# Regrouping the third gating cycle of a gated cross-attention block, with its second layer in three passes

## The chip, the cores and the metric

The kernel runs on one core of a Trainium2 chip. The metric is the device time of one execution, in microseconds (us); lower is better. A core has TensorE (PE, matrix products into the accumulator memory PSUM), VectorE (DVE), ScalarE (ACT), GpSimd (POOL) and SyncE (SP, which here only issues transfers). Each engine works through its own list of instructions in order; an instruction may wait on semaphores that other engines or transfers raise.

## The reference, cut to what matters

```python
x = x + tanh(g_xattn) * attention(layernorm(x), ctx, ctx, adj, mask, ...)     # not touched
x = x + tanh(g_ffn) * ffn(layernorm(x))

def ffn(x):                                   # 4 batches of 1024 tokens, 512 features
    gf = global_net(mean over tokens of x)    # one value a batch
    out = x
    for _ in range(3):                        # three gating cycles
        h = gelu(out @ w1 + b1)               # 512 -> 512
        h = gelu(h @ w2 + b2)                 # 512 -> 256
        h = gelu(h @ w3 + b3)                 # 256 -> 128
        tf = sigmoid(h @ w4 + b4)             # 128 -> 1
        coupling = 0.1 + adaptive_range * (0.7 * gf + 0.3 * tf - 0.5) * 2
        out = out + coupling * twist(out)     # twist turns quarters of the row, with signs
    return out
```

## The kernel before, in words

The program has three phases, one after the other on every engine: projections, attention, and the last one, `ffn_phase`, which alone is touched. It runs over four batches; a batch is worked as two streams, j = 0 and j = 1, of 512 tokens each. Arrays of a stream are tiles of 128 features x 512 tokens, four tiles to 512 features.

A batch begins with the output projection of attention (`project`, 12 products for each of 8 pieces; stream 1's piece s waits for DVE's `residual` of stream 0's piece s, since they share the accumulator), goes on with layer normalisation, transposes and the first layer (`first_layer`), and ends with the three gating cycles. Since `twist` is linear and turning twice gives the negative, the first layer is computed once: A = w1 applied to x, B = w1 applied to the twisted x. Before the first cycle's gelu the sum is A. With the coupling of the first cycle in `beta` the second cycle's sum is A + beta B. With c the coupling of the second cycle, the third cycle's sum is alpha A + (beta + c) B, alpha = 1 - beta c.

In a cycle n of stream j: DVE forms the sum tile by tile into `u[j]` (`mix`), ACT applies gelu in place (`h1`), PE multiplies by w2 (`layer2`, four tiles t, two products each), ACT applies gelu (`h2_half`, twice), PE multiplies by w3 (`layer3`), ACT applies gelu (`h3_all`), PE multiplies by w4 (`layer4`, copied to all 128 rows), ACT takes tanh (`gate`), DVE makes the coefficients (`coefficients`). PE alternates the streams: it does tiles 1, 2, 3 of a turn's `layer2`, then `layer3`, then tile 0 of the next turn's `layer2`, then `layer4`. ACT's order is fixed in `batch`: in the turn of one stream it does that stream's `h2_half` twice, `h1` tile 0 of the other stream's next cycle, `h3_all`, `h1` tile 1, `gate`, and then `h1` tiles 2 and 3. No engine can take a later instruction ahead of one that waits.

In the first cycle `layer2` is three products in the fast format for each one (`three_pass`: high x high, low x high, high x low), from a rounded copy `u_hi` that ACT writes and a low part `u_lo` that DVE's `split_u` makes; `SPLIT = 1` says that only cycle 0 does so. The other two cycles use one full-precision product, which the profile shows as two records.

After the third cycle the output is written in rows. For it the coefficients are wanted as columns: ACT packs alpha and beta into one tile (`pack`), PE turns it (`columns`), DVE reads it (`gated_columns`), makes the columns of the output (`y_columns`), and finishes it piece by piece (`finish`, or `finish_base` and `finish_add` where ACT does the twisted part in `twist`: only in the last stream of the last batch).

In batch 0 POOL also finishes the last four pieces of the attention's output (`split_weighted`, five operations each, which SP loads before and stores after), while the cycles run; only after the fourth does SP go on to load the next batch's rows.

## Time and profile before

| | us |
|---|---|
| median of three runs (lowest, highest) | 1735.72 (1734.1, 1736.67) |
| profiled execution, its own time | 1736.92 |
| its span, first to last instruction | 1735.1 |
| PE busy / DVE / ACT / POOL | 1708.5 / 1443.4 / 1244.5 / 659.9 |
| `ffn_phase`, first product of batch 0 to that of batch 1 | 1244.27 to 1367.32 |
| the same, batch 1 to batch 2 | 1367.32 to 1486.57 |

The busy time of an engine is the time in which at least one of its instructions was executing. The span starts at the first instruction; all positions below are microseconds from there. A timeline row gives an instruction's start and duration; neighbours on one engine may overlap, so that what one costs its engine is the distance from its start to the next one's.

### The profile page before, as it was taken

To read this page: it belongs to the slowest core of one execution; us is meant where nothing else is said; L and a number is where in the kernel's file an instruction comes from. 1 tells how busy PE (TensorE), PEld (TensorE's weight loads), DVE (VectorE), ACT (ScalarE), POOL (GpSimd) and SP (SyncE) were. 2 spreads that over 40 slices of the span, in tenths; PEclk is the share of its full clock that TensorE was granted. 3 is DMA by queue.
4 is the path that set the end of the run, shared out by engine and by line. 5 is a ranking of instruction groups with operands and counts; after the bars stand their busy time and mean duration, and the time that the engine had idled before them with its cause. 6 is when DMAs were issued, how large, how long until landed. Compare 5 with 4: busy or idle time off the path is not lost. (4 is left out here: it accounts for less than half of the span.)

```text
span 1735.1 us, 34186 instructions
## 1 busy us (share of the span) xinstructions
PE 1708.5 (98%) x12456; PEld 1291.2 (74%) x12456; DVE 1443.4 (83%) x2554; ACT 1244.5 (72%) x2185; POOL 659.9 (38%) x590
## 2 busy tenths in 40 slices
PE   9999999999999999999999999999999999999997
PEld 7887888777777777777777777777775685774863
DVE  6554555999999999999999999999678976868868
ACT  4222223999999999999999999999574365365455
POOL 3432341423278542586432885633235010100100
PEclk9999999999999999999999999999999999999999
DMA  7778675865468665567764686455403513221101
GB/s 279 274 239 289 225 270 158 189 184 135 131 160 198 129 154 123 135 212 142 160 154 116 185 182 138 120 111 153 162 17 98 169 40 119 88 74 49 64 1 49
DMA packets 152472, 254.65 MB, mean 147 GB/s; under 512 B 17024, under 2 KB 69504, under 8 KB 152320
## 3 DMA queue, kind: packets, MB, share of 16 engines
q1 hardware_dynamic: 101936, 158.78, 28.7%
q0 software_dynamic: 49808, 92.82, 23.8%
q8 instruction: 93, 1.52, 0.4%
q10 hardware_dynamic: 576, 1.05, 0.2%
q14 instruction: 59, 0.48, 0.1%
HBM read 168.44 MB, written 84.15 MB: 146 GB/s over the span
## 5 line engine op out<-in xcount | busy, mean ns | idle before, releaser
L1021 DVE CUSTOM_DVE_ANT_0 a_neg<-a_sc_ps,am 128x1024 f32<-128x1024 f32 x512 | 621.5, 1214 | 1.4 <-PE a_sc_ps L853 1.3
L961 ACT ACTIVATE a_prob<-a_neg,a_row_min 128x1024 f32<-128x1024 f32 x512 | 585.5, 1144 | 13.9 <-DVE a_row_min L1021 7.8
L867 PEld LDWEIGHTS a_tr_ps<-ident,a_prob 128*128 128x128 f32 x4096 | 461.0, 140 | 89.2 <-issue 53.2
L867 PE MATMUL a_tr_ps<-ident,a_prob 128*128 128x128 f32 x4096 | 519.8, 274 | 0.9 <-ACT a_probT L939 0.9
L996 DVE COPY a_probT<-a_tr_ps 128x512 f32<-128x512 f32 x512 | 350.5, 685 | 36.8 <-PE a_tr_ps L867 35.3
L939 ACT ACTIVATE a_probT<-a_tr_ps 128x512 f32<-128x512 f32 x512 | 304.0, 594 | 35.2 <-PE a_tr_ps L867 16.2
L749 POOL DMA_DIRECT2D a_q_st<-q_parts x144 | 79.4, 558 | 201.2 <-PE a_sc_ps L853 165.4
L853 PE MATMUL a_sc_ps<-k_first,a_q_st 96*128 96x512 f32 x384 | 126.3, 427 | 0.1
L853 PE MATMUL a_sc_ps<-a_k_st,a_q_st 96*128 96x512 f32 x384 | 125.8, 426 | 0.0
L887 PE MATMUL a_o_ps<-a_probT,a_v 128*32 128x256 f32 x2048 | 123.6, 382 | 0.6 <-ACT a_o L950 0.6
L887 PE MATMUL a_o_ps<-a_probT,v_first 128*32 128x256 f32 x2048 | 123.8, 382 | 0.0
L1380 PE MATMUL f_acc<-f_u,f_w 128*128 128x512 f32 x256 | 116.0, 596 | 0.7 <-ACT f_u L1517 0.7
L887 PEld LDWEIGHTS a_o_ps<-a_probT,a_v 128*32 128x32 f32 x2048 | 60.5, 109 | 55.8 <-ACT a_probT L939 12.0
L887 PEld LDWEIGHTS a_o_ps<-a_probT,v_first 128*32 128x32 f32 x2048 | 60.0, 109 | 56.2 <-DVE a_probT L996 11.6
L961 ACT ACTIVATION_READ_ACCUMULATOR a_prob<-a_neg,a_row_min 128x1 f32 x512 | 97.1, 190 | 0.0
L754 POOL TENSOR_SCALAR a_m_raw<-a_m_raw 128x1024 f32<-128x1024 int32 x24 | 86.9, 3629 | 25.4 <-DMA a_m_raw<-mask 25.4
L1380 PEld LDWEIGHTS f_acc<-f_u,f_w 128*128 128x128 f32 x256 | 47.6, 190 | 61.7 <-issue 48.5
L132 POOL TENSOR_TENSOR st_o<-st_o,st_rinv 128x512 f32<-128x512 f32 x32 | 41.6, 1300 | 110.3 <-DMA st_rinv<-rinv_all 110.2
L1670 DVE TENSOR_TENSOR f_B<-f_B,f_acc 128x512 f32<-128x512 f32 x64 | 43.7, 682 | 33.6 <-PE f_acc L166 23.8
L1274 POOL TENSOR_TENSOR f_rstd<-f_var_eps,f_minus_half 128x4 f32<-128x4 f32 x8 | 10.4, 1297 | 160.6 <-DVE f_neg_mean L1647 160.6
L488 DVE SCALAR_TENSOR_TENSOR p_out_lo<-p_acc,p_bias_k,p_out_hi 128x512 fp32r<-128x512 f32 x32 | 23.7, 750 | 55.2 <-ACT p_out_hi L416 55.2
L1521 ACT ACTIVATE f_h<-f_acc,small_b 128x512 f32<-128x512 f32 x48 | 32.8, 687 | 48.6 <-PE f_acc L1380 33.7
(227 smaller groups left out, 3166.2 us busy)
## 6 DMA issues: line engine op xcount, KB each, us to landing
a_q_st<-q_parts POOLq DMA_DIRECT2D x144, 128.0 KB, 3.9
k_first<-k_parts POOLq DMA_DIRECT2D x24, 512.0 KB, 8.3
a_k_st<-k_parts POOLq DMA_DIRECT2D x24, 512.0 KB, 8.1
a_m_raw<-mask SPq DMA_DIRECT2D x24, 512.0 KB, 5.0
a_adj_raw<-adj SPq DMA_DIRECT2D x24, 512.0 KB, 5.9
k_parts<-p_out_hi SPq DMA_DIRECT2D x32, 256.0 KB, 4.2
k_parts<-p_out_lo SPq DMA_DIRECT2D x32, 256.0 KB, 6.2
v_all<-p_v_out SPq DMA_DIRECT2D x8, 1024.0 KB, 4.4
```

The costliest lines, as they stand in the source:

```text
L132: pool.tensor_tensor(w.o[:], w.o[:], w.rinv[:], ALU.mult).then_inc(w.step, 1)
L749: pool.dma_start(q_st[qb][quad * D:(quad + 1) * D], src).then_inc(q_loaded[qb], 16)
L754: pool.tensor_scalar(m_raw[:, t % 2, :].bitcast(F32), m_raw[:, t % 2, :], 0.0, -BIG, ALU.is_equal, ALU.mult).then_inc(big_ready, 1)
L853: last = pe.matmul(sc_ps[:, r % 2, half * 512:(half + 1) * 512], q_st[qb][0:STACK, h, qt * P:(qt + 1) * P], k_st[par][0:STACK, h, half * 5 ...
L867: last = pe.transpose(tr_ps[:, bank(u, half), j * P:(j + 1) * P], prob[:, r % NPROB, t * P:(t + 1) * P], ident[:])
L887: last = pe.matmul(o_ps[h * D:(h + 1) * D, 0:QB], v_sb[vpar][:, t, h * D:(h + 1) * D], probT[:, prev % 2, h, t, :], start=(t == 0), stop=( ...
L939: act.activation(probT[:, (r // UB) % 2, h, 0:4, qt * P:(qt + 1) * P], tr_ps[:, bank(u, 0), :].rearrange("p (t q) -> p t q", t=4), ACT.Cop ...
L961: act.activation(prob[:, r % NPROB, :], neg[:, r % 2, :], ACT.Exp, scale=-1.0, bias=row_min[:, r % 2:r % 2 + 1], accum_out=row_sum[:, r // ...
L996: dve.tensor_copy(probT[:, (r // UB) % 2, h, 4:8, qt * P:(qt + 1) * P], tr_ps[:, bank(u, 1), :].rearrange("p (t q) -> p t q", t=4)).then_i ...
L1021: dve.tensor_tensor_reduce(out=neg[:, r % 2, :], in0=sc_ps[:, r % 2, :], in1=am[:, 2 * qb + qt, :], scale=-1.0, scalar=3.4e38, op0=ALU.add ...
L1380: last = pe.matmul(acc[:, 2 * j + m, :], w2[:, t, m * P:(m + 1) * P], u[j][:, t, :], start=t == 0, stop=t == ET - 1)
L1670: dve.tensor_tensor(target[j][:, m, :], target[j][:, m, :], acc[:, 2 + step // 2, :], op).then_inc(shared_read, 1)
```

## The change

It touches only `ffn_phase`. In its own parts:

1. The third cycle's sum is regrouped: the second cycle's sum A + beta B is kept in `u[j]`, B - beta A is built beside it (`turned`: per tile one product beta A and one subtraction), and the third cycle's sum is u + c (B - beta A) (`third_cycle`). So that `u[j]` survives, the second cycle's gelu goes to a tile of its own, `h1_second`.
2. The coupling is formed on ACT, by a second activation behind the tanh, instead of on DVE; alpha, `cross` and the sum beta + c of full width are gone.
3. The third cycle's `layer2` is in three passes as well (`SPLIT = (0, 2)`). ACT writes gelu twice for it (`u_hi_third` and `u`), DVE makes the low part (`split_u`).
4. The split weights are copied by two transfers from POOL's queue (`keep_w2`) to a place that the next batch's attention tiles don't overwrite; those tiles' loads (`load_attention`) now wait for the copy (stream 0) or for the batch's last `layer2` (stream 1), whose `u_hi_third` lies where they go.
5. The columns no longer go through ACT and PE. SP stores one row of beta and of c to memory and loads them back as columns; DVE makes the gated columns from them with four small operations.
6. In the turn of stream 0's third cycle ACT also does the twisted part of two of the four output pieces (`twist(b, 0, 2)`, `twist(b, 0, 3)`), in all batches.

```diff
+        w2_kept = [nc.alloc_sbuf_tensor_at(f"f_w2_kept{part}", [P, ET, F2], F32R, offset=sb.offset + 4096 * part) for part in range(2)]
...
+        u_hi_third = [nc.alloc_sbuf_tensor_at(f"f_u_hi_third{j}", [P, ET, CH], F32R, offset=SB_AM + 8192 * j) for j in range(NJ)]
...
+                for j in range(NJ):
+                    sp.wait_ge(t_ready, turn(b, 1, j) + 1)
+                    for kind, row in enumerate((beta, coef)):
+                        sp.dma_start(gate_rows[b, j, kind:kind + 1], row[0:1, j, :]).then_inc(rows_stored, 16)
+                    sp.wait_ge(rows_stored, 32 * (NJ * b + j + 1))
+                    with nc.allow_non_contiguous_dma(reason="one row becomes four columns"):
+                        for kind in range(2):
+                            sp.dma_start(raw_cols[:, j, kind], gate_rows[b, j, kind].rearrange("(s p) -> p s", p=P)).then_inc(cols_loaded[j], 16)
...
         @block.gpsimd
         def _(pool):
+            def keep_w2(b):
+                pool.wait_ge(product_ready, 4 * ET * NJ * (b + 1))
+                pool.wait_ge(w2_lo_ready, b + 1)
+                for kept, tile in zip(w2_kept, (w2_hi, w2_lo)):
+                    pool.dma_start(kept[:], tile[:]).then_inc(w2_kept_loaded, 16)
...
             def load_attention(b, j, part):
                 if j == 0:
-                    pool.wait_ge(z2_ready, 2 * turn(b - 1, SPLIT - 1, 1) + 2)
+                    pool.wait_ge(z2_ready, 2 * turn(b - 1, 0, 1) + 2)
+                    pool.wait_ge(w2_kept_loaded, 32 * b)
                 else:
...
+                keep_w2(b)
...
-                    for j in (1, 0):
+                    for j in range(NJ):
                         for part in range(2):
                             load_attention(b + 1, j, part)
...
-                    if n < SPLIT:
-                        pe.wait_ge(w2_lo_ready, b + 1)
+                    if n in SPLIT:
                         pe.wait_ge(u_lo_ready, ET * turn_split(b, n, j) + t + 1)
-                        for m in range(2):
...
+                        if n in SPLIT:
+                            last = three_pass(pe, acc[:, 2 * j + m, :], w_hi[:, t, ms], w_lo[:, t, ms], high[:, t, :], u_lo[j][:, t, :],
                                               t == 0, t == ET - 1)
-                            if t == ET - 1:
-                                last.then_inc(z2_ready, 1)
-                        continue
-                    pe.wait_ge(h1_ready, ET * k + t + 1)
-                    for m in range(2):
...
             def h1(b, n, j, m):
                 k = ((CYCLES - 1) * b + n - 1) * NJ + j
+                if n == 1:
+                    act.wait_ge(product_ready, 4 * ET * NJ * (b + 1))
+                elif m == 0:
+                    act.wait_ge(z2_ready, 2 * turn(b, 1, j) + 2)
                 act.wait_ge(u_ready, ET * k + m + 1)
-                if n < SPLIT:
-                    act.activation(u_hi[j][:, m, :], u[j][:, m, :], ACT.Gelu, bias=small.b1[:, m:m + 1])
+                if n == 1:
+                    act.activation(h1_second[j][:, m, :], u[j][:, m, :], ACT.Gelu, bias=small.b1[:, m:m + 1]).then_inc(h1_ready, 1)
+                    return
+                act.activation(u_hi_third[j][:, m, :], u[j][:, m, :], ACT.Gelu, bias=small.b1[:, m:m + 1])
...
+                if n == 0:
+                    wait(act, rows_stored, 32 * NJ * b)
+                act.activation(coef[:, j, :], z4[:, j, :], ACT.Tanh, scale=0.5, bias=small.half_b4[:]).then_inc(tanh_ready, 1)
+                act.wait_ge(base_ready, b + 1)
+                act.wait_ge(tanh_ready, NJ * ((CYCLES - 1) * b + n) + j + 1)
+                act.activation((beta if n == 0 else coef)[:, j, :], coef[:, j, :], ACT.Identity, scale=small.range_3[:], bias=base[:]).then_inc(t_ready, 1)
...
-                        if other[1] == CYCLES - 1:
-                            pack(b, other[2])
+                    if n == CYCLES - 1 and j == 0:
+                        twist(b, 0, 2)
+                        twist(b, 0, 3)
...
-                add(ET - 1)
+                    dve.tensor_tensor(u[j][:, m, :], u[j][:, m, :], A[j][:, m, :], ALU.add).then_inc(u_ready, 1)
+                in_turn(scale, add)
+            def turned(b, j, tiles):
+                k = ET * (NJ * b + j)
+                dve.wait_ge(u_ready, ET * ((CYCLES - 1) * b * NJ + j + 1))
+                for m in tiles:
+                    dve.tensor_tensor(A[j][:, m, :], A[j][:, m, :], beta[:, j, :], ALU.mult).then_inc(twist_step, 1)
+                    if m > tiles[0]:
+                        subtract(j, m - 1, k)
+                subtract(j, tiles[-1], k)
+            def subtract(j, m, k):
+                dve.wait_ge(twist_step, k + m + 1)
+                dve.tensor_tensor(Bt[j][:, m, :], Bt[j][:, m, :], A[j][:, m, :], ALU.subtract).then_inc(turned_ready, 1)
+            def third_cycle(b, j):
+                k = ET * (NJ * b + j)
+                dve.wait_ge(t_ready, turn(b, 1, j) + 1)
+                dve.wait_ge(turned_ready, k + ET)
+                def scale(m):
+                    dve.tensor_tensor(Bt[j][:, m, :], Bt[j][:, m, :], coef[:, j, :], ALU.mult).then_inc(B_scaled, 1)
+                def add(m):
+                    dve.wait_ge(B_scaled, k + m + 1)
+                    dve.tensor_tensor(u[j][:, m, :], u[j][:, m, :], Bt[j][:, m, :], ALU.add).then_inc(u_ready, 1)
+                in_turn(scale, add)
             def gated_columns(b, j):
                 k = NJ * b + j
-                dve.wait_ge(cols_ps_ready, k + 1)
-                dve.tensor_scalar(cols[:, j].rearrange("p k s -> p s k"), z4[:, j, 0:2 * TT].rearrange("p (s k) -> p s k", k=2),
-                                  small.gate_f[:], None, ALU.mult).then_inc(cols_ready, 1)
+                be, c, al, both = raw_cols[:, j, 0], raw_cols[:, j, 1], cols[:, j, 0], cols[:, j, 1]
+                dve.wait_ge(cols_loaded[j], 32 * (b + 1))
+                dve.scalar_tensor_tensor(al, be, -1.0, c, ALU.mult, ALU.mult).then_inc(cols_step, 1)
+                dve.tensor_tensor(both, be, c, ALU.add).then_inc(cols_step, 1)
+                dve.wait_ge(cols_step, 2 * k + 2)
+                dve.tensor_scalar(al, al, 1.0, small.gate_f[:], ALU.add, ALU.mult).then_inc(cols_ready, 1)
...
                 dve.wait_ge(t_ready, turn(b, CYCLES - 1, j) + 1)
                 dve.tensor_scalar(c, t_cols[:, j], small.range_3[:], base[:], ALU.mult, ALU.add).then_inc(y_cols_step, 1)
-                dve.wait_ge(cols_ready, k + 1)
+                dve.wait_ge(cols_ready, 2 * k + 2)
                 dve.wait_ge(y_cols_step, done + 1)
                 dve.tensor_tensor(cross_be, c, be, ALU.mult).then_inc(y_cols_step, 1)
                 dve.tensor_tensor(cross_al, c, al, ALU.mult).then_inc(y_cols_step, 1)
...
-                    if n < CYCLES - 1:
-                        coefficients(b, n, j)
-                        mix(b, n + 1, j)
-                        if n + 1 < SPLIT:
-                            split_u(b, n + 1, j)
+                    if n == 0:
+                        second_cycle(b, j)
+                        turned(b, 0, ((0, 1, 2), (3,))[j])
+                        if j:
+                            turned(b, 1, (0, 1))
+                    elif n == 1:
+                        third_cycle(b, j)
+                        if j == 0:
+                            turned(b, 1, (2,))
+                        split_u(b, 2, j)
+                        if j == 0:
+                            turned(b, 1, (3,))
                     else:
                         gated_columns(b, j)
                         y_columns(b, j)
                         if j == 0:
-                            for s in range(TT):
-                                finish(b, 0, s)
+                            finish(b, 0, 0)
+                            finish(b, 0, 1)
+                            finish_base(b, 0, 2)
+                            finish_base(b, 0, 3)
+                            finish_add(b, 0, 2)
+                            finish_add(b, 0, 3)
             batches(dve, batch)
```

Names in the order rows: `f_u_..02` and `..08` are u[0], the next number u[1]; `w_raw` is A of stream 1; `f_B` the B of a stream; `f_h` holds the outputs of `h2_half` and `h3_all`; f_acc, f_tr and f_z are PSUM. A row ends with the size of the output, and x2 is two alike.

ACT, last batch, the turn of stream 1's second cycle, before:

```order
L1521 ACTIVATE f_h_1_18607<-f_acc,small_b_71 128x512 x2
L1517 ACTIVATE f_u_18602<-f_u_18602,small_b_70 128x512
L1525 ACTIVATE f_h_1_18607<-f_tr,small_b_72 128x512
L1517 ACTIVATE f_u_18602<-f_u_18602,small_b_70 128x512
L1530 ACTIVATE f_coef<-f_z,small_half_b_75 128x512
L1517 ACTIVATE f_u_18602<-f_u_18602,small_b_70 128x512 x2
L1541 ACTIVATE f_coef<-f_alpha 64x512
L1542 ACTIVATE f_coef<-f_beta 64x512
```


and now:

```order
L1538 ACTIVATE f_h_1_18613<-f_acc,small_b_71 128x512 x2
L1533 ACTIVATE f_u_hi_third_18600<-f_u_18608,small_b_70 128x512
L1534 ACTIVATE f_u_18608<-f_u_18608,small_b_70 128x512
L1542 ACTIVATE f_h_1_18613<-f_tr,small_b_72 128x512
L1533 ACTIVATE f_u_hi_third_18600<-f_u_18608,small_b_70 128x512
L1534 ACTIVATE f_u_18608<-f_u_18608,small_b_70 128x512
L1549 ACTIVATE f_coef<-f_z,small_half_b_75 128x512
L1552 ACTIVATE f_coef<-f_coef,f_base,small_range_77 128x512
L1533 ACTIVATE f_u_hi_third_18600<-f_u_18608,small_b_70 128x512
L1534 ACTIVATE f_u_18608<-f_u_18608,small_b_70 128x512
L1533 ACTIVATE f_u_hi_third_18600<-f_u_18608,small_b_70 128x512
L1534 ACTIVATE f_u_18608<-f_u_18608,small_b_70 128x512
```


Behind the two activations of `h2_half` stood eight instructions (four gelus, `h3_all`, the tanh and two of packing); now there are eleven (eight gelus, `h3_all`, the tanh and the second activation of the gate), and the last two of these stand before the gelus of tiles 2 and 3. The twists of part 6 come in the next turn, behind the gelus of stream 1's tiles 2 and 3 and ahead of stream 1's `h2_half`.

DVE, last batch, stream 1's third sum (all but its first two operations) and the first operation of stream 0's columns, before:

```order
L1707 TENSOR_TENSOR f_u_18603<-w_raw,f_alpha 128x512
L1708 TENSOR_TENSOR f_B_18601<-f_B_18601,f_beta 128x512
L1715 TENSOR_TENSOR f_u_18603<-f_u_18603,f_B_18601 128x512
L1707 TENSOR_TENSOR f_u_18603<-w_raw,f_alpha 128x512
L1708 TENSOR_TENSOR f_B_18601<-f_B_18601,f_beta 128x512
L1715 TENSOR_TENSOR f_u_18603<-f_u_18603,f_B_18601 128x512
L1707 TENSOR_TENSOR f_u_18603<-w_raw,f_alpha 128x512
L1708 TENSOR_TENSOR f_B_18601<-f_B_18601,f_beta 128x512
L1715 TENSOR_TENSOR f_u_18603<-f_u_18603,f_B_18601 128x512 x2
L1727 TENSOR_SCALAR f_cols<-f_z,small_gate_f 128x4x2
```


and now, the stretch from the last pieces of `turned` to the low parts of stream 1:

```order
L1724 TENSOR_TENSOR w_raw<-w_raw,f_beta 128x512
L1731 TENSOR_TENSOR f_B_18607<-f_B_18607,w_raw 128x512
L1695 TENSOR_TENSOR f_u_lo_18610<-f_u_18608,f_u_hi_third_18600 128x512 x4
L1724 TENSOR_TENSOR w_raw<-w_raw,f_beta 128x512
L1731 TENSOR_TENSOR f_B_18607<-f_B_18607,w_raw 128x512
L1739 TENSOR_TENSOR f_B_18607<-f_B_18607,f_coef 128x512 x2
L1743 TENSOR_TENSOR f_u_18609<-f_u_18609,f_B_18607 128x512
L1739 TENSOR_TENSOR f_B_18607<-f_B_18607,f_coef 128x512
L1743 TENSOR_TENSOR f_u_18609<-f_u_18609,f_B_18607 128x512
L1739 TENSOR_TENSOR f_B_18607<-f_B_18607,f_coef 128x512
L1743 TENSOR_TENSOR f_u_18609<-f_u_18609,f_B_18607 128x512 x2
L1695 TENSOR_TENSOR f_u_lo_18611<-f_u_18609,f_u_hi_third_18601 128x512 x4
```


Stream 1's third sum used to follow stream 0's with only the coefficients between, and the columns followed it; now it stands behind four low parts of stream 0 and one more pair of `turned`, and four low parts of stream 1 stand between it and the columns.

POOL, batch 0, before (`f_rstd` and `f_shift` belong to the normalisation of stream 1, `st_` tiles to `split_weighted`):

```order
L1276 TENSOR_TENSOR f_shift<-f_neg_mean,f_rstd 128x4
L1269 TENSOR_TENSOR f_pair_lo<-f_alpha,f_pair_hi 128x512 x2
L132 TENSOR_TENSOR st_o<-st_o,st_rinv 128x512
L135 TENSOR_SCALAR st_lo<-st_o 128x512
L137 TENSOR_TENSOR st_hi<-st_lo,st_o 128x512
```


and now:

```order
L1289 TENSOR_TENSOR f_rstd<-f_var_eps,f_minus_half 128x4
L1291 TENSOR_TENSOR f_shift<-f_neg_mean,f_rstd 128x4
L1284 TENSOR_TENSOR f_pair_lo<-f_pair_raw,f_pair_hi 128x512 x2
L1262 DMA f_w_kept_18594<-f_w_hi 128x1024
L1262 DMA f_w_kept_18595<-f_w_lo 128x1024
L132 TENSOR_TENSOR st_o<-st_o,st_rinv 128x512
L135 TENSOR_SCALAR st_lo<-st_o 128x512
```


The two copies of the weights stand before the first of the four splits, and they wait for the last first-layer product of the batch.

## Rows read from the trace of the kernel before

**Rows 1.** Page, parts 1 and 2: busy time, and the granted clock in tenths.

```profile
PE 1708.5 (98%) x12456; PEld 1291.2 (74%) x12456; DVE 1443.4 (83%) x2554; ACT 1244.5 (72%) x2185; POOL 659.9 (38%) x590
...
PEclk9999999999999999999999999999999999999999
```

**Rows 2.** Busy time of each engine in the stretches of batch 0 and batch 1.

```profile
core 0: us, PE busy (x) PEld busy (x) DVE busy (x) ACT busy (x) POOL busy (x), PEclk, DMA share, GB/s
1244.00:1367.00 123.00, 118.65 (x468) 80.35 (x468) 98.76 (x164) 67.22 (x117) 43.21 (x35) 1.00 0.34 106
1367.00:1486.00 119.00, 118.11 (x470) 80.55 (x470) 91.32 (x186) 63.34 (x113) 11.10 (x12) 1.00 0.25 77
```

**Rows 3.** Timeline, PE, batch 1: start us, us, instruction, [idle before <-releaser].

```profile
1457.54 5.31 PE L1380 MATMUL f_acc<-f_u,f_w 128*128 128x512 f32 x12
1462.77 1.99 PE L1388 MATMUL f_tr<-f_h,f_w 128*128 128x512 f32 x4
...
1464.61 1.98 PE L1380 MATMUL f_acc<-f_u,f_w 128*128 128x512 f32 x4
...
1472.44 0.95 PE L1409 MATMUL f_z<-ident,f_coef 128*128 128x2 f32 x8
1473.25 1.96 PE L1388 MATMUL f_tr<-f_h,f_w 128*128 128x512 f32 x4
...
1476.77 0.95 PE L1402 MATMUL f_tr<-small_w_col,f_h 128*128 128x1 f32 x8
...
1484.71 0.95 PE L1409 MATMUL f_z<-ident,f_coef 128*128 128x2 f32 x8
```

**Rows 4.** Timeline, PE, batch 1, first and last of 17 three-pass products in a row.

```profile
1439.36 0.39 PE L165 MATMUL f_acc<-f_u_hi,f_w_lo 128*128 128x512 f32 x1
...
1443.02 0.39 PE L166 MATMUL f_acc<-f_u_lo,f_w_hi 128*128 128x512 f32 x1
```

**Rows 5.** Timeline, ACT: batch 0 normalisation, batch 1 cycles, last twists.

```profile
1382.62 2.94 ACT L1471 ACTIVATE f_xn<-x,f_shift,f_rstd 128x512 f32<-128x512 f32 x4 [14.86 <-POOL f_shift L1276]
...
1457.74 0.69 ACT L1530 ACTIVATE f_coef<-f_z,small_half_b 128x512 f32<-128x512 f32 x1 [1.28 <-PE f_z L1396]
1458.32 1.32 ACT L1517 ACTIVATE f_u<-f_u,small_b 128x512 f32<-128x512 f32 x2
...
1462.89 0.69 ACT L1521 ACTIVATE f_h<-f_acc,small_b 128x512 f32<-128x512 f32 x1 [0.17 <-PE f_acc L1380]
...
1726.44 3.61 ACT L1549 ACTIVATE f_B<-f_xn,f_y_cols 128x128 f32<-128x128 f32 x12 [0.97 <-DVE f_y_cols L1745]
```

**Rows 6.** Timeline, DVE, batch 1, third cycle and columns.

```profile
1460.70 0.69 DVE L1707 TENSOR_TENSOR f_u<-f_A,f_alpha 128x512 f32<-128x512 f32 x1
1461.31 0.68 DVE L1708 TENSOR_TENSOR f_B<-f_B,f_beta 128x512 f32<-128x512 f32 x1
...
1477.69 0.22 DVE L1727 TENSOR_SCALAR f_cols<-f_z,small_gate_f 128x8 f32<-128x8 f32 x1
...
1479.30 0.75 DVE L1750 SCALAR_TENSOR_TENSOR f_u<-f_xn,f_y_cols,x 128x512 f32<-128x512 f32 x1
```

**Rows 7.** Timeline, batch 0: PE, POOL (first and last operation of splits) and DVE.

```profile
1306.06 0.39 PE L166 MATMUL f_acc<-f_pair_lo,f_w_hi 128*128 128x512 f32 x1
...
1304.03 1.29 POOL L132 TENSOR_TENSOR st_o<-st_o,st_rinv 128x512 f32<-128x512 f32 x1 [5.80 <-DMA st_rinv<-rinv_all]
...
1330.52 1.39 POOL L132 TENSOR_TENSOR st_o<-st_o,st_rinv 128x512 f32<-128x512 f32 x1 [7.17 <-DMA st_rinv<-rinv_all]
...
1336.36 1.59 POOL L141 TENSOR_TENSOR st_lo<-st_o,st_hi 128x512 f32<-128x512 f32 x1
...
1330.70 1.75 DVE L1715 TENSOR_TENSOR f_u<-f_u,w_raw 128x512 f32<-128x512 f32 x1
```

**Rows 8.** Transfers of the last phase: KB each, median us from issue to landing.

```profile
X_lo<-att_parts POOLq DMA_DIRECT2D x6, 1024.0 KB, 8.2
...
st_rinv<-rinv_all SPq DMA_DIRECT2D x12, 64.0 KB, 2.9
```

More of the change, by code:

```diff
@@ L1529, in gate @@
                 act.wait_ge(z4_ready, turn(b, n, j) + 1)
-                act.activation(coef[:, j, :], z4[:, j, :], ACT.Tanh, scale=0.5, bias=small.half_b4[:]).then_inc(t_ready, 1)
+                if n == 0:
[4 more added lines that the diff above has]
+                act.activation((beta if n == 0 else coef)[:, j, :], coef[:, j, :], ACT.Identity, scale=small.range_3[:], bias=base[:]).then_inc(t_ready, 1)
             def gate_columns(b, j):
@@ L1710, in add, with in_turn, second_cycle @@
+            def in_turn(first, second):
+                first(0)
+                for m in range(1, ET):
+                    first(m)
+                    second(m - 1)
+                second(ET - 1)
+            def second_cycle(b, j):
+                k = ET * (NJ * b + j)
+                dve.wait_ge(t_ready, turn(b, 0, j) + 1)
+                def scale(m):
+                    dve.tensor_tensor(u[j][:, m, :], Bt[j][:, m, :], beta[:, j, :], ALU.mult).then_inc(mul_ready, 1)
                 def add(m):
```

103 lines of the change are left out of this document (37 added, 66 removed).

## The prediction

> **What bounds the kernel now.** I read the page first. PE is busy 98% of the span at full granted clock [rows 1], so what counts is PE's own work and what it waits for. Then the windows of the last phase: from batch 1 on, PE is busy 118.11 of 119 us; in batch 0, 118.65 of 123 [rows 2]. The reader is to see that nearly nothing waits there now, so that every microsecond taken from PE is won and every new wait is lost, and that batch 0 already pays some 4 us more than a later one. Last, the timelines of batch 1's cycles on PE, ACT and DVE [rows 3 to 6], for the distances at which the engines hand a tile to each other: PE does not wait there because a tile is ready just in time, not because much is in hand.
>
> **What the change removes from PE, per batch.** A full-precision tile of `layer2` takes (1462.77 - 1457.54)/3 = 1.74 us [rows 3]. A three-pass tile is six products at (1443.02 - 1439.36)/16 = 0.229 us, 1.37 [rows 4]. Eight tiles of the third cycle: 8 x 0.37 = 2.9 us. The two `columns` go: 0.81 (1473.25 - 1472.44) and 0.95 [rows 3]. Together 4.6 us a batch.
>
> **What it adds, followed down the chain of one batch.** Prices: a DVE operation of 128x512 occupies DVE 0.60 us and its result is there after 0.68 [rows 6]; a gelu occupies ACT 0.61 and is done after 0.71; the tanh is done after 0.69; an activation with scale and bias in columns, which the trace has in the normalisation, occupies (2.94 - 0.81)/3 = 0.71 [rows 5], the 0.81 being its own length, taken slightly above the gelu's. A handing over costs about 0.03.
>
> (a) Second activation of the gate. In batch 1 the tanh starts at 1457.74 and the gelu of tile 2 at 1458.32 [rows 5]. PE began tile 1 at 1457.54 and wants tile 2 at 1459.28 [rows 3]; the gelu is done at 1459.03, so 0.25 in hand. The second activation must await the tanh's end (1458.43) and takes 0.71, so tile 2 starts 0.83 later: a wait of 0.6, once in each stream's second cycle, 1.2.
>
> (b) Stream 0, third cycle, tile 0. The second `h2_half` starts at 1462.89 and ACT is free 0.6 later [rows 5]. Two gelus, done at 1464.8, then the low part, 1465.5. PE has finished `layer3` at 1464.5 (its next product starts at 1464.61 [rows 3]). Wait 1.0.
>
> (c) Stream 0, tile 2. It stands behind the gate of stream 1, which awaits `layer4`. From `layer4`'s end: 0.2 until the tanh (1457.54 to 1457.74), 0.69, 0.71, 0.61, 0.71, 0.68 and handings, 3.7. PE has only tile 1 to do meanwhile, 1.37 now where it was 1.74. Wait 2.3.
>
> (d) Stream 1, tile 0. DVE is in order and its low parts of stream 0 hang on (c). From the start of the low part of tile 3: it, a pair of `turned` with two awaited results, and eight operations of the third sum (0.6 + 1.4 + 4.8), then the low part of stream 1's tile 0, 0.7: 7.5. PE has from there 0.7 until it may begin, 1.4 for tile 3, 0.2 for `h2_half`, 1.8 for `layer3`: 4.1. Wait 3.4.
>
> (e) Stream 1, tile 2: 0.2 + 0.2 for the tanh of four columns, 0.61 + 0.71 + 0.68, 2.4 against tile 1's 1.37. Wait 1.0.
>
> (f) Stream 1's `h2_half` now stands behind eight twists, which await the columns of stream 0, which DVE makes behind stream 1's last low part. From that low part's start: 0.6, the columns 1.6 before (1477.69 to 1479.30 [rows 6]) and 2.0 with three more small operations, twists 8 x 3.61/12 = 2.4 [rows 5], first `h2_half` 0.7: 5.7. PE has 0.7 + 1.4. Wait 3.5.
>
> (g) The last four products await `h3_all`, 0.2 + 0.69, which the second `columns` covered. Wait 0.9.
>
> Sum 1.2 + 1.0 + 2.3 + 3.4 + 1.0 + 3.5 + 0.9 = 13.3; less 4.6, **8.7 us a batch, 35 in four**.
>
> **Batch 0 besides.** POOL's splits of attention output keep DVE back: beside them a DVE operation on two SBUF tiles took 1.75 instead of 0.68 [rows 7]; a split lasts 1330.52 to 1337.95, seven microseconds, and they come every (1330.52 - 1304.03)/2 = 13.2, the first at about 1291. `keep_w2` puts two issues of 0.8 ahead of the first, which await the last first-layer product, 1306.06 [rows 7]. So they start at about 1308, 1321, 1334 and 1347. Where one fell on idle DVE, the last three now lie on the second and third sums, where (d) has no room: four or five held operations each at 1.07 more, 4.7 x 3 = 14. Batch 0 paid 4 before [rows 2]. I take +10. Bounds: nothing, if the holding were hidden as one of the four was, and 16, if the late end of the splits (about 1354, then SP's loads of two x 1 MB and only then the columns) keeps DVE waiting too.
>
> The SBUF page of the Trainium skill ("SBUF — State Buffer", on the engine ports) calls the port pair that DVE and GpSimd share an exclusive lock held for a whole instruction, the loser fully blocked. By that each held DVE operation would cost a whole POOL operation, 1.29 us, and batch 0 some 3 us more. The row, 1.07, decides for the sum.
>
> **What I cost at nothing.** The copies of the weights: issued at the batch's middle, needed over 20 us later; a 1 MB transfer beside another lands in 8.2 [rows 8]. Stream 1's attention tiles, now issued behind the last `layer2`: 0.8 + 8.2, while PE has `layer3`, waits and 48 products x 0.229 = 11 ahead. The columns' way through memory: nothing here has rows of single elements; from below two times 2.9 (the 64 KB loads [rows 8]), from above 2.9 + 8.2 = 11; they leave when the gate of stream j's second cycle is done and are read about 15 us later, behind the low parts. If any of them lost its cover, it would cost its lateness in every batch, up to some 3 us. DVE's `turned` before the third cycle falls into idle time.
>
> **Sum.** 35 + 10 = 45 on the profiled execution's own 1736.9, 1782; the median lies 1.2 below it. I predict **1781 us**. Ends: (a) to (g) each read off distances good to about 0.3, two of them long chains, so 6.5 to 11 a batch, 26 to 44; batch 0, 0 to 16. So 1762 to 1796 for this case.
>
> **Rivals.**
> - *Not slower: the in-order queues hold nothing that PE wants* (0.06). Faster if the waits stay under 4.6 a batch; with none, 1735.7 - 18 = 1717. For it: ACT and DVE are busy only 63 and 91 of 119 us [rows 2], enough room on average. Against: (b) and (c) alone make 3.3 from single distances, and (d) hangs on (c). It decides only if tile 2 of stream 0 comes within 1.4 us of `layer4`, less than the two parts of the gate take.
> - *Half of it* (0.09): the queues wait, but (d) or (f) overlap with other waits and batch 0's holding hides; 4 a batch and 3, 1755.
> - *The clock falls* (0.09). Granted clock is full now [rows 1], with PE never idle long; after, it stands still for 3 us several times within 25, and for up to 9 in batch 0. If it went to the lower of its two levels, 1.2 GHz, in the third cycle, PE's 15 us there (11 for the tiles, 3.5 for `layer3`) would double, half of that hidden by waits: +7 a batch, 1810. The page "TensorE: Matmul & The Clock Gate" of the Trainium skill (Part 1) says just this, that an idle stretch halves the clock until the array has been busy again. For the forecast it speaks that full idleness never lasts here but in batch 0.
> - *Late transfers* (0.05): columns or attention tiles arrive 3 us late in each batch, 1793.
> - *The waits as summed* (0.71).
>
> A measurement of this kernel tells about 0.2% (3.5 us) from no change. Faster 0.05 and same 0.01 come from the first rival, another 0.01 of same from the low end of the second; slower 0.93. The range is that of the forecast, with a little of its neighbours: 1758 to 1799.
>
> **What would show it.** In the trace after: PE's three-pass tiles at 1.37 in the third cycle and no `columns` rows (part 1). PE idle 2 us and more ahead of stream 0's tile 2 and 3 us and more ahead of stream 1's tile 0, both released by DVE's low part; PE ahead of stream 1's `layer3` idle 3 us, released by ACT's `h2_half`, which stands behind twists. A batch-to-batch distance near 128 instead of 119.25, and near 141 for the first. Wrong would be: less than 1.5 us at tile 2 (then the gate is cheaper than its rows say), a granted clock under full, DVE waiting for transfers at the columns, or a first batch that loses no more than the others.

## The result, and the profile after

The changed kernel takes 1786.59 us, median of 4 runs (1781.41 to 1788.67), the kernel before 1736.2 beside it: a ratio of 1.0286, 95% interval 1.0273 to 1.0299. It is slower, by 50 us where 45 were forecast; 1786.59 lies inside the range. The profiled execution took 1787.3 us, its span is 1785.5. From the page, parts 1 and 2:

```profile
PE 1713.9 (96%) x12456; PEld 1303.1 (73%) x12456; DVE 1464.7 (82%) x2578; ACT 1277.5 (72%) x2249; POOL 668.9 (37%) x598
PEclk9999999999999999999999999999998999998998
```

Against [rows 1] PE is busy for a smaller share, and the granted clock has digits of 8 in its last quarter, one or two to a batch. The first product of each batch (output projection) starts at 1243.69, 1382.96, 1513.02 and 1644.15: distances of 139.3, 130.1 and 131.1 us, and 141.3 from the last one to the end of the span. Before they were 123.0, 119.2, 119.2 and 129.3. So the loss is 16.2 in batch 0 and 10.8, 11.9 and 12.0 in the others.

Timeline of PE in batch 1, the rows with a wait (start us, us, instruction, [idle before <-releaser]); they answer to [rows 3], where no such row has one:

```profile
1476.55 3.70 PE L1400 MATMUL f_acc<-f_h_second,f_w 128*128 128x512 f32 x8 [0.58 <-ACT f_h_second L1531]
...
1483.08 0.47 PE L164 MATMUL f_acc<-f_u_hi_third,f_w_kept 128*128 128x512 f32 x1 [0.92 <-DVE f_u_lo L1695]
...
1489.19 0.50 PE L164 MATMUL f_acc<-f_u_hi_third,f_w_kept 128*128 128x512 f32 x1 [2.25 <-DVE f_u_lo L1695]
...
1490.86 0.63 PE L164 MATMUL f_acc<-f_u_hi_third,f_w_kept 128*128 128x512 f32 x1
1491.29 0.63 PE L165 MATMUL f_acc<-f_u_hi_third,f_w_kept 128*128 128x512 f32 x1
...
1497.45 0.47 PE L164 MATMUL f_acc<-f_u_hi_third,f_w_kept 128*128 128x512 f32 x1 [1.92 <-DVE f_u_lo L1695]
...
1502.18 0.50 PE L164 MATMUL f_acc<-f_u_hi_third,f_w_kept 128*128 128x512 f32 x1 [0.82 <-DVE f_u_lo L1695]
...
1507.81 3.51 PE L1408 MATMUL f_tr<-f_h,f_w 128*128 128x512 f32 x4 [2.60 <-ACT f_h L1538]
...
1512.10 1.05 PE L1422 MATMUL f_tr<-small_w_col,f_h 128*128 128x1 f32 x8 [0.78 <-ACT f_h L1542]
```

Waits (a), once of its two, to (g) stand there in their order with the releasers the prediction named. The two rows at 1490.86 and 1491.29 are 0.43 us apart where such products were 0.229 apart [rows 4]: the clock has fallen. The windows of PE (us, busy (x), granted clock, DMA share, GB/s) show it after each longer wait:

```profile
1385.00:1487.00 102.00, 98.89 (x403) 1.00 0.25 77
1487.00:1489.00 2.00, 0.00 (x0) 1.00 0.01 2
...
1491.00:1495.00 4.00, 4.00 (x11) 0.64 0.01 2
1495.00:1505.00 10.00, 7.26 (x34) 1.00 0.00 1
...
1507.00:1511.00 4.00, 3.19 (x4) 0.57 1.10 327
```

A part of the rival on the clock is thus true beside the forecast. DVE and ACT show why (d) and (f) last. For (d): behind the last low part of stream 0 come a pair of `turned` and the eight operations of stream 1's third sum, and only then the low part that PE awaits. For (f): the twists await DVE's columns, and `h2_half` stands behind them.

```profile
1490.28 0.68 DVE L1724 TENSOR_TENSOR w_raw<-w_raw,f_beta 128x512 f32<-128x512 f32 x1
1491.00 0.69 DVE L1731 TENSOR_TENSOR f_B<-f_B,w_raw 128x512 f32<-128x512 f32 x1
...
1496.61 0.69 DVE L1695 TENSOR_TENSOR f_u_lo<-f_u,f_u_hi_third 128x512 fp32r<-128x512 f32 x1
...
1504.54 0.16 DVE L1773 SCALAR_TENSOR_TENSOR f_y_cols<-f_cross_cols,f_cols 128x4 f32<-128x4 f32 x1
...
1504.73 2.46 ACT L1564 ACTIVATE f_B<-f_xn,f_y_cols 128x128 f32<-128x128 f32 x8 [2.10 <-DVE f_y_cols L1773]
1507.09 1.25 ACT L1538 ACTIVATE f_h<-f_acc,small_b 128x512 f32<-128x512 f32 x2
```

### The profile page after: what moved, and what is told of

It is laid out like the page before. It is cut to its first block and busy times, and to the rows that moved or that the text cites. A ratio compares the mean times of both kernels' runs of the same rounds, so it can differ in the third digit from the quotient of the medians.

```text
span 1785.5 us, 34360 instructions
## 1 busy us (share of the span) xinstructions
PE 1713.9 (96%) x12456; PEld 1303.1 (73%) x12456; DVE 1464.7 (82%) x2578; ACT 1277.5 (72%) x2249; POOL 668.9 (37%) x598
## 5 line engine op out<-in xcount | busy, mean ns | idle before, releaser
L853 PE MATMUL a_sc_ps<-k_first,a_q_st 96*128 96x512 f32 x384 | 126.5, 427 | 0.1
L853 PE MATMUL a_sc_ps<-a_k_st,a_q_st 96*128 96x512 f32 x384 | 126.2, 427 | 0.0
L887 PE MATMUL a_o_ps<-a_probT,a_v 128*32 128x256 f32 x2048 | 123.6, 382 | 0.6 <-ACT a_o L950 0.6
L887 PEld LDWEIGHTS a_o_ps<-a_probT,v_first 128*32 128x32 f32 x2048 | 60.0, 109 | 56.3 <-DVE a_probT L996 11.9
L1480 ACT ACTIVATE f_xn<-x,f_shift,f_rstd 128x512 f32<-128x512 f32 x32 | 23.5, 808 | 61.3 <-POOL f_shift L1291 61.3
L416 ACT ACTIVATE p_out_hi<-p_acc,p_bias_q 128x512 fp32r<-128x512 f32 x32 | 22.0, 690 | 62.1 <-PE p_acc L166 62.1
L402 ACT ACTIVATE p_c_hi<-p_c_raw 128x2048 fp32r<-128x2048 f32 x7 | 13.4, 1919 | 73.4 <-PE p_acc L166 58.6
```

The lines of the kernel that those rows point to most:

```text
L853: last = pe.matmul(sc_ps[:, r % 2, half * 512:(half + 1) * 512], q_st[qb][0:STACK, h, qt * P:(qt + 1) * P], k_st[par][0:STACK, h, half * 5 ...
L887: last = pe.matmul(o_ps[h * D:(h + 1) * D, 0:QB], v_sb[vpar][:, t, h * D:(h + 1) * D], probT[:, prev % 2, h, t, :], start=(t == 0), stop=( ...
```

## The experiments

All are the changed kernel with an edit. A batch distance is that from the first product of a batch to the first of the next. Two theories stand against each other for batches 1 to 3: the waits that in-order queues make (the prediction's sum, 8.7 us a batch), and the clock; for batch 0 the held DVE operations and the transfers are in question. The kernel before beside these runs was 1735.4 to 1736.2 us; intervals are 95%.

**Filler in the waits.** Is the fallen clock a cost of its own?

```
+ def keep_busy(count):
+     for _ in range(count):
+         pe.matmul(z4[:, 0, :], wo_hi[:, 0, 0:P], wo_hi[:, 1, :], start=True, stop=True)
  # ahead of stream 0's tiles 0 and 2: 2 and 8; stream 1's: 8 and 3; its layer3: 10
```

> PE runs 33 single-pass products with an unused result per batch (some 7.5 us at full clock) in the third cycle's waits, no more in any than it lasted; nothing else is changed, and the reference's result is kept. If the fallen clock (0.72 to 0.91 granted in the stretches behind the waits) costs time beyond the waits themselves, the clock stays at 0.99 and the later three batches are 2 to 3 us shorter each (128 us as summed from the waits alone), 1775 to 1781 us. If products at half clock only take up what would be waited for anyway, the time stays within 2 us of 1786.6; if the filler delays products that were ready, it is 2 to 5 us more.

1779.34 us, ratio 1.0249 (1.0232 to 1.0267), 6.4 us less than the changed kernel by the two ratios. Batch distances 139.5, 128.3, 128.4 and 138.0 to the end; windows of PE:

```profile
1383.00:1511.30 128.30, 122.84 (x503) 87.19 (x503) 96.39 (x194) 71.06 (x129) 12.24 (x14) 1.00 0.26 79
1511.30:1639.60 128.30, 122.84 (x503) 87.16 (x502) 96.39 (x194) 71.06 (x129) 12.20 (x14) 1.00 0.26 79
```

The clock (after PEld, DVE, ACT and POOL) is 1.00 and the batches are 1.7, 2.8 and 3.3 us shorter, though PE does 31 products more that nobody reads (2 + 8 + 8 + 3 + 10, not the 33 of the expectation). So the clock costs 7.8 us in three batches of the profiled executions (6.4 in the whole by the medians), and what is left, 9.1, 9.2 and 8.7 above before, is the waits' part: 8.7 was forecast. PE's rows say where the clock's part lies:

```profile
1507.62 1.98 PE L1416 MATMUL f_tr<-f_h,f_w 128*128 128x512 f32 x4 [0.33 <-ACT f_h L1546]
1510.38 1.05 PE L1430 MATMUL f_tr<-small_w_col,f_h 128*128 128x1 f32 x8 [0.78 <-ACT f_h L1550]
```

From this `layer3` to the next batch it is 3.7 us (1507.62 to 1511.30); in the changed kernel, at the fallen clock, 5.2 in batch 1 (1507.81 to 1513.02) and 6.3 in batch 2. The other slow stretch, behind wait (c), costs next to nothing: PE is later, but only for a tile that isn't ready, and (d) is the shorter for it.

**ACT's order: gelus ahead of the gate.**

```
+ early = between and other[1] == CYCLES - 1
+ if early:
+     h1(*other, 2); h1(*other, 3)
  gate(b, n, j) / gate_columns(b, j)
- if between:
+ if between and not early:
      h1(*other, 2); h1(*other, 3)
```

> In ACT's third-cycle turns the gelus of tiles 2 and 3 (two for each tile now) run ahead of the gate's tanh and scaling. If ACT's queue order makes the waits before tiles 2 of both streams and, through DVE's low parts, before stream 1's tile 0, then the waits before tile 2 (2.25 and 0.8 us) go and the one before stream 1's tile 0 shrinks by no more than is lost by the later gate: a batch is 5 to 6 us shorter (124 to 125 us instead of 130 to 131) and the time is 1757 to 1766 us. If these waits are set by DVE's amount of work or by the clock, the later gate delays DVE's third sum of stream 1 by 2.5 us and the time is 1786 to 1796 us.

1770.13 us, ratio 1.0208 (1.0184 to 1.0233). Batches 1 and 2 are 123.1 and 122.2 us, better than expected, but the time misses the 1766 by 4. Of batch 1's waits (c) and (e) are gone, (d) is 2.62, and (f) is gone too, since the twists' columns no longer await the late low parts. Batch 0 grew to 147.0. From its timelines:

```profile
1361.82 0.51 SPq L1210 DMA_DIRECT2D f_x_rows<-x_bo  x1
1362.37 0.40 SPq L1242 DMA_DIRECT2D gate_rows<-f_beta  x1
...
1371.16 0.94 SPq L1246 DMA_DIRECT2D f_raw_cols<-gate_rows  x2
...
1379.72 0.16 DVE L1756 SCALAR_TENSOR_TENSOR f_cols<-f_raw_cols 128x4 f32<-128x4 f32 x1 [11.77 <-DMA f_raw_cols<-gate_rows]
...
1381.18 2.44 ACT L1564 ACTIVATE f_B<-f_xn,f_y_cols 128x128 f32<-128x128 f32 x8 [13.81 <-DVE f_y_cols L1777]
...
1384.25 3.78 PE L1408 MATMUL f_tr<-f_h,f_w 128*128 128x512 f32 x4 [14.04 <-ACT f_h L1538]
```

2 KB of gate rows left at 1362.4 behind the row loads of 1 MB, took until 1371 to be stored and until 1379.7 to come back as columns; DVE, then ACT, then PE stood 12 to 14 us. ACT's order settles batches 1 to 3; batch 0 has a second bound just behind the first.

**The same, and SP exchanges stream 0's rows ahead of the loads in batch 0.**

```
+ if first:
+     exchange(b, 0)        # the gate rows' two stores and two loads
  if more: ... load_x(b + 1, j)
- for j in range(NJ): exchange
+ for j in range(first, NJ): exchange(b, j)
```

> The gelus of the third cycle's tiles 2 and 3 run ahead of the gate, as in the run that had this alone, and in the first batch SP exchanges stream 0's gate rows before it issues the loads of the next batch's rows. If that run's wait of 14 us in its first batch came from the columns' transfer behind 4 MB of loads (DVE waited 11.8 us for it, and ACT's gated copies stood behind DVE), it shrinks to under 3 us and the time is 1755 to 1762 us, 8 to 13 us under that run. If the transfer was late for another reason, or the loads of x that are issued later are missed instead, the time stays at 1767 to 1773 us with a wait of the same size at the first batch's end or the second's start.

1759.47 us, 1.0134 (1.0117 to 1.0151), 12.8 less by the ratios. Batch 0 is 136.4, its wait 3.61 (a little over the 3 expected), the others 123.0 and 123.1. The transfer was the cause.

**POOL's order: the weights' copies behind the splits.** `keep_w2(b)` moves below the loop of `split_weighted`.

> POOL's two copies of the second layer's weights are issued behind the splits of the attention output instead of ahead of them; only the first batch changes. If the splits, begun later by the wait ahead of the copies, hold DVE and so PE in the first batch (the 10 us of the prediction's step on batch 0), the first batch is 4 to 10 us shorter than the 138.7 us of the changed kernel, the wait of 7.95 us before 1352.4 shrinks by as much, later batches stay at 130 to 131, and the time is 1777 to 1782 us. If batch 0 is longer for another reason (the three-pass layer and the fallen clock), the time stays within 2 us of 1786.6 us and the wait stays at 8.

1782.44 us, 1.026 (1.024 to 1.0281): 4.5 us less, with an uncertainty as large. The time lies between the two expectations. The last split's store leaves SP at 1336.9 instead of 1356.5, yet batch 0 is only 1.1 shorter (138.2): the wait of 7.95 is 3.87, (d) came back at 3.15, and so did one of 2.03 that the kernel before has too (2.17). The late splits alone are not the extra.

**DVE without beta A and B minus beta A.** It leaves out `turned`, so the third cycle gates B itself.

> DVE leaves out the 16 operations per batch that form beta A and B minus beta A (so the third cycle gates B itself, another result); all else stays. If they are hidden, as the prediction's step that costs them at nothing has it, batches after the first are unchanged within 0.5 us and only the first, where POOL's splits slow each of them, is shorter: 0 to 5 us, 1781 to 1787 us. If their 11 us of DVE time per batch stand in a queue that PE waits for, batches after the first are 1 to 2 us shorter and the time is 1766 to 1776 us.

1785.58 us, 1.0287 (1.027 to 1.0304): no less in all, but the batches aren't what "hidden" would make them. Their distances are 143.2, 129.6, 126.9 and 138.8: batch 0 is 4.0 longer, the others 0.5, 4.2 and 2.6 shorter. PE's rows of batch 1:

```profile
1494.27 0.49 PE L164 MATMUL f_acc<-f_u_hi_third,f_w_kept 128*128 128x512 f32 x1 [2.25 <-DVE f_u_lo L1695]
...
1501.01 0.47 PE L164 MATMUL f_acc<-f_u_hi_third,f_w_kept 128*128 128x512 f32 x1 [1.63 <-DVE f_u_lo L1695]
```

From tile 2 of stream 0 to tile 0 of stream 1 it is 6.7 us, where the changed kernel has 8.3 (1489.19 to 1497.45): the pair of `turned` that stands in chain (d) is 1.5 us of it. The prediction's sum has that pair at 1.4; the expectation here left it out of account. Waits (b) and (c) are the same (0.91 and 2.25), so the operations ahead of the third cycle are hidden there. Batch 2 ran at a granted clock of 1.00 throughout and is 1.4 us under the 128.4 of the run with filler, which had 1.00 too; the rest of the gain is clock that did not fall in the third cycles of batches 1 and 2, though their waits of 2.25 and 2.61 are those of the changed kernel. Batch 1 gave most of it back, since its first 4 us, behind a wait of 13.85, ran at 0.50.

The timelines of DVE in batch 0 say more. In the changed kernel:

```profile
1336.50 1.64 DVE L1731 TENSOR_TENSOR f_B<-f_B,f_A 128x512 f32<-128x512 f32 x1
1338.07 2.77 DVE L1724 TENSOR_TENSOR w_raw<-w_raw,f_beta 128x512 f32<-128x512 f32 x2
1340.76 3.42 DVE L1731 TENSOR_TENSOR f_B<-f_B,w_raw 128x512 f32<-128x512 f32 x2
1344.10 1.28 DVE L1739 TENSOR_TENSOR f_B<-f_B,f_coef 128x512 f32<-128x512 f32 x2
```

and without them:

```profile
1335.57 2.37 DVE L1738 TENSOR_TENSOR f_B<-f_B,f_coef 128x512 f32<-128x512 f32 x2 [4.50 <-ACT f_coef L1552]
...
1374.64 0.16 DVE L1751 SCALAR_TENSOR_TENSOR f_cols<-f_raw_cols 128x4 f32<-128x4 f32 x1 [11.15 <-DMA f_raw_cols<-gate_rows]
```

The gate's coefficient was there at 1337.39 + 0.82 = 1338.2, and DVE took it up at 1344.1, 5.9 us later, behind `turned` operations that started 1.0 to 1.7 us apart beside POOL's (0.6 without them). With the weights' copies behind the splits, where POOL did not hold them, it was still 3.2 us (coefficient at 1339.76, third sum at 1342.92). Left out, the wait before the third cycle's tile 0 fell from 7.95 to 1.56, and the columns' transfer took it all back: 13.85 us before `layer3`.

**Twists back on DVE.** The two `twist` calls of stream 0 go from ACT; DVE runs `finish` for all four row tiles.

> Stream 0's gated copies of row tiles 2 and 3 go from ACT back to DVE, as in the kernel before. If every wait of PE adds to the time by itself (as the prediction's sum has it), the wait before stream 1's third layer in the third cycle (2.6 us here, 3.5 forecast) goes in four batches, 10 to 14 us: 1773 to 1777 us. If DVE, which takes 3 us more of work at the end of a batch, is as late as PE, the wait goes from there and stands again at the start of the next batch before the first transposes of the normalised rows: a batch is 0 to 1 us shorter and the last one some 3 us longer at its end, 1783 to 1789 us.

1778.18 us, 1.0238 (1.0221 to 1.0255): 8.3 less, between the two expectations. (f) is gone from every batch; in its stead the wait before `first_layer` grew from 0.55 to 1.1 to 1.3, (d) was 3.15 or 1.67, and batches were 129.6 and 126.5. Of the 10.4 us that (f) took in four batches about 8 were to be had.

**Useful work in the waits.**

```
  layer3(b, n, j)
+ if more and k == NJ * CYCLES - 2:
+     project(b + 1, 0, 0)      # ahead of stream 1's tile 0
```

and `project(b + 1, 0, 1)` ahead of the last `layer3`.

> PE gets useful work for two waits: row tile 0 of the next batch's output projection (2.8 us) stands before stream 1's tile 0 of the third cycle, and row tile 1 before stream 1's third layer; nothing is added or left out. If each wait of PE is lost time by itself, 1.9 to 2.8 us in each of two places and the fallen clock behind them come back in three batches, 12 to 20 us: 1767 to 1775 us. If DVE, behind in the same stretch, is as late as PE, the waits come again at the next batch's start, before the transposes of its normalised rows (up to 2.9 us there), and only about 1.5 us a batch and the clock's part are won: 1774 to 1782 us.

1774.66 us, 1.0221 (1.0204 to 1.0238), 11.3 less; batch distances 125.5 and 126.5. Both waits are gone, and this row is new in each later batch (timeline, PE, start of batch 2):

```profile
1525.09 1.07 PE L1332 MATMUL f_tr<-ident,f_xn 128*128 128x128 f32 x8 [2.47 <-issue]
1526.00 1.56 PE L1332 MATMUL f_z<-ident,f_xn 128*128 128x128 f32 x8
1527.20 0.77 PE L164 MATMUL f_acc<-wo_hi,X_hi 128*128 128x512 f32 x1
1527.78 0.63 PE L165 MATMUL f_acc<-wo_hi,X_lo 128*128 128x512 f32 x1
```

The normalised rows come late from DVE, and the clock falls there instead (the products behind them start 0.43 us apart). The time lies where both expectations overlap; the rows show both at work, filled waits and a new one.

**One full product in the third cycle.** `SPLIT = (0,)`: one gelu a tile, no low parts; everything else of the change stays.

> The third cycle's second layer goes back to one full product for each tile and half (1.74 us a tile on PE), so that ACT has one gelu a tile there and DVE no low parts; the regrouping, the two steps of the gate on ACT, the columns by transfers and stream 0's gated copies on ACT stay. If the three passes' helpers (8 gelus and 8 low parts per batch) make the waits before the tiles in the third cycle, a batch after the first is 120 to 122 us and the time is 1749 to 1757 us, two thirds or more of the loss gone; what is left is the first batch's. If the regrouping, the gate on ACT or the columns make the loss, the time stays at 1770 us or above, since PE has 2.9 us more a batch.

1763.29 us, 1.0159 (1.0142 to 1.0176). Batches 1 and 2 are 121.0, so the three-pass layer, which was to take 2.9 us a batch off PE, costs 9 to 10 net, the clock's part in it. The time misses the 1757 expected by 6: batch 0 is 144.3, with 15.64 us before its last `layer3` behind the columns.

**The same with the rows ahead.** The edit of SP as above.

> One full product per tile and half in the third cycle, as in the run that had this alone (1763.3 us, whose first batch of 144.3 us ended with a wait of 15.6 us behind the columns' transfer), and in the first batch SP exchanges stream 0's gate rows before the loads of the next batch's rows. If that wait is the transfer's, queued behind those loads, the first batch is 128 to 134 us, later ones 121.0 as they are, and the time is 1749 to 1755 us; if it is not, 1760 us or more.

1758.88 us, 1.0132 (1.0117 to 1.0148): missed. Batch 0 is still 142.2, and batch 1 is 123.6 instead of 121.0, with a granted clock of 0.50 in its first 4 us. Timelines of POOL, SP and DVE:

```profile
1367.43 0.74 POOL L1277 DMA_DIRECT2D X_hi<-att_parts  x1 [8.32 <-PE f_acc L1405]
...
1367.59 0.94 SPq L1223 DMA_DIRECT2D f_raw_cols<-gate_rows  x2
...
1375.12 0.16 DVE L1755 SCALAR_TENSOR_TENSOR f_cols<-f_raw_cols 128x4 f32<-128x4 f32 x1 [14.01 <-DMA f_raw_cols<-gate_rows]
```

PE, now ahead, released POOL's attention tiles 0.16 us before the columns left, on another queue; the columns took 7.5 us, where in the run with both orders, whose tiles left at 1370.8, they had landed 2.7 us after their issue. In the three other runs whose columns left behind such tiles (0.7 us behind with the gelus ahead, 1.2 without `turned`, 5.3 with one product) they took 8.6, 7.8 and 5.5 us; with the twists on DVE and with filler, where the tiles left later, 2.7. So SP's order was only one way into that traffic.

**Orders together.** Gelus ahead of the gate, copies behind the splits, rows ahead, and the gate's scaling on DVE (`tensor_scalar` in `coefficient`).

> All of the change with its three-pass layer, but four places in other order: the gelus of the third cycle's tiles 2 and 3 ahead of the gate, the weights' copies behind POOL's splits, stream 0's gate rows ahead of the loads in the first batch, and the gate's scaling on DVE again (0.5 us there for 0.8 us on ACT). From the run that had the first and third (1759.5 us, batches 136.4, 123.0, 123.1): the scaling takes away two waits of 0.58 us a batch and 0.3 us of another, so batches after the first are 121 to 122.5 us; the copies behind the splits take 1 to 6 us of the first. Together 1748 to 1756 us if ACT's and POOL's queue orders are what is lost; if DVE is the bound in the third cycle, its 0.5 us for each gate come back as longer waits and the time is 1757 to 1762 us.

1755.06 us, 1.0113 (1.0097 to 1.0128): the time is in the range, its parts are not. Batch 0 fell to 131.3, but the others are 123.7 where 121 to 122.5 were expected, longer than the 123.0 of the run with both orders, although all waits of one sum to 5.6 us where batch 2 of that run had 6.3. The clock has it: of batch 1's windows

```profile
1482.50:1486.50 4.00, 1.92 (x7) 0.87 0.02 0
1486.50:1490.50 4.00, 4.00 (x15) 0.50 0.00 0
1490.50:1494.50 4.00, 3.90 (x15) 0.77 0.01 2
```

Its waits are 1.27 and 2.64 us.

**These and row tile 0 of the next projection.**

> The four orders of the run before the last, and row tile 0 of the next batch's projection (2.8 us of PE) in the wait of 2.6 us that is left before stream 1's tile 0. If DVE has room at the next batch's start, nearly all of that wait is filled: three batches 2 to 2.5 us shorter, 5 to 7 us less than the four orders alone. If it has not, the wait comes again before the transposes and the gain is 0 to 3 us.

1744.65 us, 1.0051 (1.0035 to 1.0066), 10.8 less than without it, more than the 5 to 7 expected. A batch's first product now stands in the batch before, so the distances are taken here from first product of the first layer to the next: 130.6, 118.8 and 119.1, where the run without it has 131.4, 123.7 and 123.6. Thus 2.8 us of work in a wait of 2.6 brought 4.8 and 4.5 in batches 1 and 2. The waits of one sum to 4.1 us instead of 5.6; the rest is the clock, which is 1.00 all through them. With the three-pass layer this is the best; the kernel before has 123.2, 119.2 and 119.2, so what is left of the loss is in batch 0 and in the last batch.

**One product, no copies.** The third cycle has one full product; POOL makes no copies of the weights, the gate's scaling is on DVE, and stream 0's rows go ahead of the loads in batch 0. The gelus stay behind the gate.

> The regrouping and the columns by transfers with one full product in the third cycle, without copies of the weights, with the gate's scaling on DVE and stream 0's rows ahead of the loads in the first batch. PE then has 0.81 and 0.95 us less a batch than the kernel before (the columns) and none of the waits of 0.58 us: a batch after the first is 118.2 to 118.8 us against 119.2, and the first 123 to 130 us against 123. If the transfers and POOL hold nothing in the first batch, 1733 to 1736 us, at most 0.2% under the kernel before; if DVE's 16 more operations in the first batch, each slowed by POOL, hold it, 1738 to 1743 us.

1736.79 us (11 runs) against 1736.0 (15 runs), 1.0004 (0.9995 to 1.0013): no difference, and between the two expectations. Batches of 126.2, 118.5 and 118.4: 0.8 less than before in each later one, and 3.1 more in batch 0, where a wait of 2.63 us is left (that of 2.21 the kernel before has too, at 2.17).

## Why the prediction was right, and where not

**Removed from PE.** The `columns` are gone, as said. A three-pass tile takes 1.37 only behind products of its own kind: in the run with filler the tile behind the small `layer4_columns` takes 1.48 (first product at 1499.55, last at 1500.80 and 0.23 more), and the one behind a full product 1.75 (1484.91 to 1486.66). In its batch 1 the eight tiles take 12.2 us, not 11.0. Some of the 4.6 is thus not won.

**Waits (a) to (g).** Forecast 0.6 twice, 1.0, 2.3, 3.4, 1.0, 3.5, 0.9. Measured in batch 1: 0.58 twice, 0.92, 2.25, 1.92, 0.82, 2.60, 0.78. Five terms are right within 0.2. (d) is 1.92 because PE came to it late at half clock; where it came at full clock it is 3.13 to 3.15 (runs with the projection and the twists). (f) was mis-sized: from the start of the last low part (1502.66) the columns are done in 2.07 us, not 2.6, twists and `h2_half` follow in 2.4 + 0.7, and PE is busy until 1505.21, 2.55 us and not 2.1. The waits at full clock sum to 11.7, not 13.3, and with filler the net is 9.1, 9.2 and 8.7, for 8.7 forecast. By difference the removal is then worth 2.6, not 4.6: two errors, of 1.6 and 2.0 us, cancel in the net, which is luck. The tiles explain 1.2 of the missing 2.0; the rest was not traced. The run with the gelus ahead shows which queue makes (c), (e) and (f): ACT's. (d) stays there at 2.62, and the run without `turned` shows it as DVE's chain.

**The clock.** The step that failed is "full idleness never lasts here but in batch 0". The granted clock fell to its lower level of 1.2 GHz after waits of 2.25 and 2.60 us, in each of the three batches, and the filler puts it at 7.8 us in three. The rival's mechanism is real, at 1.7 to 3.3 a batch instead of 7, since the slow stretch behind (c) is covered by (d) and the one behind (f), 3.7 us long at full clock, is the last of the batch. The Trainium skill, "TensorE: Matmul & The Clock Gate", Part 1, has the rule that an idle array falls to half clock until it has been busy again. The trace agrees where the clock fell, and shows it at waits as short as these; but it did not fall behind each such wait, as batches 1 and 2 without `turned` show. In batch 0 it fell too (0.50 in the 4 us from 1352 on, behind the wait of 7.95); what that cost was not separated, and the filler left batch 0 at 139.5.

**Batch 0.** Forecast 8.7 + 10, measured 16.2, so the size is nearly right, and its reason only half. Held operations are nearly as priced: most take 1.63 to 1.78 us where 0.68 is free, 1.0 more (1.07 forecast). The Trainium skill, "SBUF — State Buffer", Terms, has the loser blocked for the whole instruction, which would be the 1.29 of POOL's operation; the trace shows less. The splits started within 2.5 us of where the forecast put them, and the second and third held DVE 4.7 and 4.6 us, as in the sum. But sixteen of its operations were held in all, against twelve in the kernel before, so the change adds only four. The shift of the splits alone is worth 1.1 us. The step that failed is that `turned` costs nothing: in batch 0 the third sum starts 5.9 us behind its coefficient because of it, 3.2 where nothing holds it. The columns' transfer, also costed at nothing, holds PE there for 12.5 to 15.6 us in four of the runs in which something else got faster, and for 3.6 in a fifth. In batches 1 to 3 the columns are free, as said: in batch 1 DVE runs them at 1503.27 with no wait for a transfer. So is the `turned` ahead of the third cycle; the pair behind stream 0's low parts is the one that (d) has at 1.4, and it measured 1.5.

**Sum.** 16.2 + 10.8 + 11.9 + 12.0 = 50.9, of which 0.6 had been won ahead of batch 0, against 45: the waits right within 0.9 in three batches, the clock's 7.8 missing, batch 0 put 2.5 too high. What is still open is why the clock falls behind a wait in one batch and not in the next. Batch distances in one kernel differ by up to 3 us with it (129.6 and 126.5 with the twists on DVE, where it fell behind (d) in the one and behind (c), covered by (d), in the other); what sets it off was not tried.

## What to carry to other kernels

Where PE hardly waits, an edit that saves its work by giving two other in-order engines a longer chain for each tile is priced by the chain, tile by tile: here 2.9 us of products saved cost 9 to 10. A wait of 2 to 3 us can cost more than itself, since the products behind it may run at half clock; it does so where no later wait covers them, and there 2.8 us of real work put into it won 4.5 to 4.8. In a first or last round with other traffic, look for the second bound behind the first before expecting a gain.

## What the runs showed of the hardware

Waits of 2.25 to 2.64 us between busy stretches could be enough for the clock to fall to 0.50 to 0.66 in 4 us behind them (0.66 from 1489.19 on, 0.57 from 1507 on, 0.50 from 1486.5 on with the orders together). They did not always do it: without `turned`, batch 2 has waits of 0.91, 2.25, 1.63, 0.83 and 2.60 and a clock of 1.00, and with waits of 0.9 and 2.6 it stayed at 1.00 in batch 1 of the run with both orders and fell to 0.72 in batch 2 (from 1611.5 on). Two transfers of 2 KB landed in 2.7 us, and in 7.5 when a load of 1 MB on another queue had been issued 0.16 us ahead of them. POOL is held by DVE as well: a multiplication that took 1.31 us (at 1307.39, beside DVE's sums with one source in PSUM) took 4.39 beside DVE's sums and `turned` of batch 0.

```profile
1333.21 4.39 POOL L132 TENSOR_TENSOR st_o<-st_o,st_rinv 128x512 f32<-128x512 f32 x1 [5.11 <-DMA st_rinv<-rinv_all]
```
